# A message-passing kernel on one core: the dot product over vector components moves from the scatter matmuls to VectorE

## The reference

```
h = relu(layernorm(x))                       # then per node: xs (64), xv (32 x 3), two small linear maps
w = silu(edge_embed @ fc_w1 + b1) @ fc_w2 + b2          # 192 weights per edge: 64 + 64 + 32 + 32
m0_a = w_ss * xs[src] * sh0                              # 64 scalars
m1_a = (w_sv * xs[src])[:, :, None] * sh1[:, None, :]    # 64 vectors
m1_b = w_vs[:, :, None] * xv[src] * sh0                  # 32 vectors
m0_b = w_vv * einsum('emc,ec->em', xv[src], sh1) / sqrt(3)   # 32 scalars: a dot product over c
agg = segment_sum(concat(m0_a, m0_b, m1_a, m1_b), dst)
out = x + h + gated(agg @ W2 + h @ Wsc)      # W2_s: 96 x 96, W2_v: 96 x 32, silu gates
```

## Time and profile before

| | |
|---|---|
| median of 3 runs | 825.63 us (825.25 to 831.32) |
| the profiled execution, whole | 822.46 us |
| its span, first to last instruction | 820.8 us |
| TensorE passes | 5900 |
| TensorE matmul busy, weight load busy | 648.3 us, 544.9 us |
| VectorE, GpSimd, ScalarE busy | 348.5 us, 405.1 us, 183.8 us |
| mean granted TensorE clock | 0.543 of full speed |

### The profile page before, as it was taken

How to read it: one execution, slowest core, us unless ns; L and a number is a source line. 1 busy time by engine, 2 the same in 40 slices (tenths; PEclk the granted TensorE clock), 3 DMA queues, 4 the chain that set the end, 5 groups by cost and what they waited for, 6 DMA issues and landing times.

```text
span 820.8 us, 16769 instructions
## 1 busy us (share of the span) xinstructions
PE 648.3 (79%) x5900; PEld 544.9 (66%) x5900; DVE 348.5 (42%) x1126; ACT 183.8 (22%) x357; POOL 405.1 (49%) x434
## 2 busy tenths in 40 slices
PE   6656776877797797797789789779778978977877
PEld 6535665666676686686577668668667766866766
DVE  7412444433454443444345434434343443444435
ACT  4611112212121212112212212121221221212121
POOL 2374555545554644554554455545556455544630
PEclk9755556555655555555555555555555555555657
DMA  9621111112111211211211211112212121111210
GB/s 297 165 71 41 52 49 53 46 50 57 48 49 49 65 40 49 63 41 49 57 44 48 53 48 52 52 42 57 56 46 54 45 57 48 49 53 44 57 39 13
DMA packets 38783, 48.10 MB, mean 59 GB/s; under 512 B 9908, under 2 KB 31443, under 8 KB 38379
## 3 DMA queue, kind: packets, MB, share of 16 engines
q0 software_dynamic: 20160, 34.33, 15.8%
q1 hardware_dynamic: 18193, 13.46, 5.5%
q10 hardware_dynamic: 410, 0.07, 0.1%
HBM read 40.67 MB, written 4.00 MB: 54 GB/s over the span
## 4 chain that ended last, share of the span: by engine, by line
PE 59%; another core or an unknown queue 17%; issue 11%; DVE 7%; DVEq 1%; ACT 0%; ACTq 0%
PE ps L701 20%; PE ps L691 15%; PE ps L682 7%; PE ps L696 7%; PE ps L733 3%; PE ps L697 2%; DVE agg L592 2%; DVE P L555 2%; PE ps L726 2%; PE ps L731 1%; PE ps L727 1%; PE ps L673 1%; DVE M L535 1%; DVEq L577 1%
## 5 line engine op out<-in xcount | busy, mean ns | idle before, releaser
L463 POOL DMA_INDIRECT gath<-table,src_sb x416 | 396.4, 953 | 362.1 <-DVE P L555 255.2
L701 PE MATMUL ps<-S,P 128*64 128x32 f32 x2496 | 294.7, 289 | 60.6 <-issue 60.1
L701 PEld LDWEIGHTS ps<-S,P 128*64 128x64 f32 x2496 | 273.2, 218 | 67.3 <-issue 66.8
L696 PE MATMUL ps<-S,P 128*64 128x48 f32 x832 | 180.9, 317 | 55.4 <-DVE agg L592 53.8
L696 PEld LDWEIGHTS ps<-S,P 128*64 128x64 f32 x832 | 122.3, 206 | 102.7 <-DVE agg L592 60.2
L691 PE MATMUL ps<-fc_sb,hid 64*128 64x192 f32 x832 | 180.8, 557 | 9.1 <-issue 8.6
L697 PE MATMUL ps<-S,P 128*64 128x16 f32 x832 | 148.2, 256 | 10.1 <-issue 10.1
L496 ACT ACTIVATE hid<-ps,fb_sb 128x256 f32<-128x256 f32 x104 | 49.4, 475 | 450.0 <-PE ps L682 294.9
L691 PEld LDWEIGHTS ps<-fc_sb,hid 64*128 64x128 f32 x832 | 121.2, 311 | 43.4 <-issue 42.6
L550 DVE TENSOR_TENSOR P<-ps,gath 128x512 f32<-128x512 f32 x103 | 71.0, 690 | 167.8 <-PE ps L691 63.0
L697 PEld LDWEIGHTS ps<-S,P 128*64 128x64 f32 x832 | 136.5, 222 | 6.1 <-issue 5.6
(11 more groups left out here) (90 smaller groups left out, 260.9 us busy)
## 6 DMA issues: line engine op xcount, KB each, us to landing
gath<-table,src_sb POOLq DMA_INDIRECT x416, 3.5
agg<-zeros SPq DMA_DIRECT2D x3, 1024.0 KB, 12.4
emb<-emb_t SPq DMA_DIRECT2D x104, 24.0 KB
out<-res SPq DMA_DIRECT2D x24, 78.1 KB
x_sb<-x SPq DMA_DIRECT2D x5, 350.0 KB
table<-prod SPq DMA_DIRECT2D x3, 420.0 KB
sh_sb<-sh_t SPq DMA_DIRECT2D x1, 840.0 KB, 8.0
table<-prod SPq DMA_DIRECT2D x1, 280.0 KB
```

What stands on the lines that cost most here:

```text
L463: nc.gpsimd.indirect_dma_start(gath[:, u, j, :], None, table, bass.IndirectOffsetOnAxis(ap=src_sb[:, t:t + 1], axis=0)).then_inc(landed, 16)
L696: nc.tensor.matmul(oj[0:64, :, 0:3], pj[:, 64:128], sj[:, :, 1:4], start=True, stop=True)
L701: ins = nc.tensor.matmul(oj[64:128, :, c:4:3 - c], pj[:, lo:lo + 64], sj[:, :, 0:2 + c:1 + c], start=(c == 0), stop=(c == NC - 1), skip_gr ...
```

## The change

The selectors S get a fifth column, the bare match, and `sh` is laid out as (x, y, z, scalar). VectorE computes for each edge the dot product of the gathered vectors with x, y, z: a multiplication into `xsh` (384 elements per partition) and a sum over the components into `dot` (128 elements), in a new function `dots` that stands between the adds and the products of a step and does not wait for the weights. P shrinks to 256 columns: `w_ss xs`, `w_sv xs`, `w_vs xv` for three components, and `w_vv dot`. The scatter of a tile takes four matmuls: two write partitions 0 to 63, two write partitions 64 to 127, in alternating order, and none accumulates. The sums of the vectors lie in other partitions than before, so the output weights `wo_v` are laid out four times over, and `sums_part` still has four matmuls, two of them now with 64 output columns in place of 32. The separate tile M of matches is gone, and with it a wait on `p_S`; waits on `p_xsh` and `p_dot` are new.

```diff
--- before.py
+++ after.py
-PC = 320
+PC = 256
...
-        wo_v = sb("wo_v", [VD, V0])
+        wo_v = sb("wo_v", [128, 2, 2, V0])
...
-        M = sb("M", [128, QT, WIN])
-        S = sb("S", [128, 2, QT, WIN, 4])
+        S = sb("S", [128, 2, QT, WIN, 5])
...
-            (wo_v[:, :], w2v), (wo_s[0:S0, :], w2s[0:S0, :]), (wo_s[96:128, :], w2s[S0:96, :]),
+            (wo_v[0:VD, 0, 0, :], w2v), (wo_v[96:128, 0, 1, :], w2v[S0:VD, :]),
+            (wo_v[0:S0, 1, 0, :], w2v[0:S0, :]), (wo_v[S0:VD, 1, 1, :], w2v[S0:VD, :]),
+            (wo_s[0:S0, :], w2s[0:S0, :]), (wo_s[96:128, :], w2s[S0:96, :]),
...
+                nc.gpsimd.memset(wo_v[:, :, :, :], 0.0)
...
-                nc.vector.memset(ps[64:96, 0:4, 0:2 * NTN], 0.0).then_inc(s_pz, 1)
+                nc.vector.memset(ps[64:128, 6, 0:QT * WIN * AC], 0.0)
+                nc.vector.memset(ps[64:128, 0:4, 0:QT * WIN * AC], 0.0).then_inc(s_pz, 1)
...
+        xsh = sb("xsh", [128, QT, NC, V0])
+        dot = sb("dot", [128, QT, V0])
...
-                    def matches(q):
-                        t = q * QT
-                        if not (isinstance(q, int) and q == 0):
-                            dve.wait_ge(p_S, q)
-                        nc.vector.tensor_tensor(M[:, :, :], iota[:, :].unsqueeze(1).broadcast_to([128, QT, WIN]),
-                                                dstrel[:, bass.ds(t, QT)].unsqueeze(2).broadcast_to([128, QT, WIN]),
+                    def matches(q, u):
+                        nc.vector.tensor_tensor(S[:, u % 2, :, :, 4],
+                                                iota[:, :].unsqueeze(1).broadcast_to([128, QT, WIN]),
+                                                dstrel[:, bass.ds(q * QT, QT)].unsqueeze(2).broadcast_to([128, QT, WIN]),
                                                 ALU.is_equal).then_inc(p_M, 1)

                     def selectors(q, u):
                         dve.wait_ge(p_M, q + 1)
                         nc.vector.tensor_tensor(
-                            S[:, u % 2, :, :, :], M[:, :, :].unsqueeze(3).broadcast_to([128, QT, WIN, 4]),
+                            S[:, u % 2, :, :, 0:4], S[:, u % 2, :, :, 4].unsqueeze(3).broadcast_to([128, QT, WIN, 4]),
                             sh_sb[:, bass.ds(q * QT, QT), :].unsqueeze(2).broadcast_to([128, QT, WIN, 4]),
                             ALU.mult).then_inc(p_S, 1)

+                    def dots(i, q, u, j0=0, j1=QT):
+
+                        if not (isinstance(i, int) and q == NQ - 1):
+                            dve.wait_ge(p_gath[u], (i + 1) * (16 * QT))
+                        nc.vector.tensor_tensor(
+                            xsh[:, j0:j1, :, :], gath[:, u, j0:j1, S0:D].rearrange("p j (c m) -> p j c m", c=NC),
+                            sh_sb[:, bass.ds(q * QT + j0, j1 - j0), 0:NC].unsqueeze(3).broadcast_to([128, j1 - j0, NC, V0]),
+                            ALU.mult).then_inc(p_xsh, 1)
+                        dve.wait_ge(p_xsh, q + 1 + j0)
+
+                        if not (isinstance(q, int) and q == 0 and j0 == 0):
+                            dve.wait_ge(p_prod, q + j0)
+                        nc.vector.tensor_reduce(dot[:, j0:j1, :], xsh[:, j0:j1, :, :].rearrange("p j c m -> p j m c"),
+                                                AX.X, ALU.add).then_inc(p_dot, 1)
+
                     def products(i, q, u):
-                        dve.wait_ge(p_gath[u], (i + 1) * (16 * QT))
                         dve.wait_ge(p_w, q + 1)
                         w, g, pu = w_ps(u), gath[:, u, :, :], P[:, u % 2, :, :]
                         nc.vector.tensor_tensor(pu[:, :, 0:128].rearrange("p j (a m) -> p j a m", a=2),
                                                 w[:, :, 0:128].rearrange("p j (a m) -> p j a m", a=2),
                                                 g[:, :, 0:S0].unsqueeze(2).broadcast_to([128, QT, 2, S0]), ALU.mult)
-                        for a in range(2):
-                            lo = 128 + V0 * a
-                            ins = nc.vector.tensor_tensor(
-                                pu[:, :, 128:PC].rearrange("p j (c a m) -> p j c a m", c=NC, a=2)[:, :, :, a, :],
-                                w[:, :, lo:lo + V0].unsqueeze(2).broadcast_to([128, QT, NC, V0]),
-                                g[:, :, S0:D].rearrange("p j (c m) -> p j c m", c=NC), ALU.mult)
-                        ins.then_inc(p_prod, 1)
+                        nc.vector.tensor_tensor(
+                            pu[:, :, 128:128 + VD].rearrange("p j (c m) -> p j c m", c=NC),
+                            w[:, :, 128:160].unsqueeze(2).broadcast_to([128, QT, NC, V0]),
+                            g[:, :, S0:D].rearrange("p j (c m) -> p j c m", c=NC), ALU.mult)
+                        dve.wait_ge(p_dot, q + 1)
+                        nc.vector.tensor_tensor(pu[:, :, 128 + VD:PC], w[:, :, 160:WN], dot[:, :, :],
+                                                ALU.mult).then_inc(p_prod, 1)

                     def last_products(j):
                         u = SLOTS - 1
                         dve.wait_ge(p_last[j], 16)
+                        dots(NI - 1, NQ - 1, u, j, j + 1)
                         dve.wait_ge(p_w, NQ)
                         w, g, pj = w_ps(u)[:, j, :], gath[:, u, j, :], P[:, u % 2, j, :]
                         nc.vector.tensor_tensor(
@@ -568,10 +591,12 @@
                             w[:, 0:128].rearrange("p (a m) -> p a m", a=2),
                             g[:, 0:S0].unsqueeze(1).broadcast_to([128, 2, S0]), ALU.mult)
                         nc.vector.tensor_tensor(
-                            pj[:, 128:PC].rearrange("p (c a m) -> p c a m", c=NC, a=2),
-                            w[:, 128:WN].rearrange("p (a m) -> p a m", a=2).unsqueeze(1).broadcast_to([128, NC, 2, V0]),
-                            g[:, S0:D].rearrange("p (c m) -> p c m", c=NC).unsqueeze(2).broadcast_to([128, NC, 2, V0]),
-                            ALU.mult).then_inc(p_prod, 1)
+                            pj[:, 128:128 + VD].rearrange("p (c m) -> p c m", c=NC),
+                            w[:, 128:160].unsqueeze(1).broadcast_to([128, NC, V0]),
+                            g[:, S0:D].rearrange("p (c m) -> p c m", c=NC), ALU.mult)
+                        dve.wait_ge(p_dot, NQ + j)
+                        nc.vector.tensor_tensor(pj[:, 128 + VD:PC], w[:, 160:WN], dot[:, j, :],
+                                                ALU.mult).then_inc(p_prod, 1)
...
-                                matches(q + 2)
+                                matches(q + 2, u)
...
+                        dots(i, q, u)
                         products(i, q, u)
...
-                        nc.tensor.matmul(oj[0:64, :, 0:3], pj[:, 64:128], sj[:, :, 1:4], start=True, stop=True)
-                        nc.tensor.matmul(oj[0:64, :, 3], pj[:, 0:64], sj[:, :, 0], start=True, stop=True)
-
-                        for c in range(NC):
-                            lo = 128 + 64 * c
-                            ins = nc.tensor.matmul(oj[64:128, :, c:4:3 - c], pj[:, lo:lo + 64], sj[:, :, 0:2 + c:1 + c],
-                                                   start=(c == 0), stop=(c == NC - 1), skip_group_check=True)
+                        nc.tensor.matmul(oj[0:64, :, 0:3], pj[:, 64:128], sj[:, :, 0:3], start=True, stop=True)
+                        nc.tensor.matmul(oj[64:128, :, 0], pj[:, 128:192], sj[:, :, 3], start=True, stop=True)
+                        nc.tensor.matmul(oj[0:64, :, 3], pj[:, 0:64], sj[:, :, 3], start=True, stop=True)
+
+                        ins = nc.tensor.matmul(oj[64:128, :, 1:4:2], pj[:, 192:PC], sj[:, :, 3:5], start=True, stop=True)
                         return ins

                     def scatter(q, u):
...
                         nc.tensor.matmul(o[:, 0:96], sums[3], wo_s[:, :], start=False, stop=False, skip_group_check=True)
-                        for k in range(NC):
-                            ins = nc.tensor.matmul(o[:, 96 + V0 * k:96 + V0 * (k + 1)], sums[k][0:VD, :], wo_v[:, :],
-                                                   start=False, stop=(k == NC - 1), skip_group_check=True)
+                        nc.tensor.matmul(o[:, 96:160], sums[0], wo_v[:, 0, :, :].rearrange("p a k -> p (a k)"),
+                                         start=False, stop=False, skip_group_check=True)
+                        nc.tensor.matmul(o[:, 128:192], sums[1][0:VD, :],
+                                         wo_v[0:VD, 1, :, :].rearrange("p a k -> p (a k)"),
+                                         start=False, stop=False, skip_group_check=True)
+                        ins = nc.tensor.matmul(o[:, 160:192], sums[2][0:S0, :], wo_v[0:S0, 0, 0, :],
+                                               start=False, stop=True, skip_group_check=True)
...
-    sh = np.pad(a["edge_attr_4"], ((0, pad + QT * TE), (0, 0)))
+
+    sh = np.pad(a["edge_attr_4"][:, [1, 2, 3, 0]], ((0, pad + QT * TE), (0, 0)))
```

(8 more changed lines are left out.)

## The result

The changed kernel takes 847.62 us (median of 4 runs, 841.63 to 848.83) against 825.44 us before (4 runs, 823.17 to 831.32): ratio 1.028, 95% interval 1.021 to 1.035. It is slower; the forecast was 720 us, range 702 to 772.

A forecast was written before the change was run, and what follows sets the result against it. It took TensorE to be bound at one pass per 0.134 us on average. From the profiled 822.5 us, minus 111 for passes, plus 4 and 2, gave 717; adjusted to the runs' median, 720 us, range 702 to 772.

The forecast's parts named there:

- the first term of the sum: TensorE's scatter: 832 of 5900 passes fewer, at an average 0.134 us per pass with stops included, 111 us less.
- GpSimd: ... Nothing: Gathers, 5.0 us per quad: above TensorE's 4.2 but under the average step of 5.9, so no cost.
- the scatter: TensorE's scatter of one step after the change: length near 1.8 us, against 2.57 before.
- the reduction: VectorE's new sum of 384 elements into 128 per step: 0.57 us, bounds 0.28 and 1.14.
- VectorE's step: VectorE's step without a wait after the change: 4.15 us, against TensorE's 4.2.
- Its share: VectorE's busy share of the span after the change: near 55%, from 42%.
- The streams' saving: TensorE's two scatter streams, four passes per tile each: 0.77 us less per step, 80 us over 104 quads.
- Rival B: TensorE's stops keep their number and length; only the streams' 80 us come out: 762 us, chance 0.28.
- Rival C: The scatter's two halves do not run side by side; 53 us saved: 777 us, chance 0.08.
- D: VectorE becomes the bound if the strided sum costs 1.4 us: no change, 825 us, chance 0.07.
- E: Selectors at 20-byte steps make TensorE's scatter passes take twice 0.107 us: 88 us more, 914 us, chance 0.05.
- Slower: Whole kernel slower by over 1%: chance 0.05.

The follow-up runs named there:

- e12: Kernel before, GpSimd waiting for free slots only at every second quad, so gathers go in runs of 8: 908.78 us, ratio 1.103.
- e7: Kernel before with every second gather left out, products reading old rows: 592.67 and 619.85 us where the kernel before takes 820.87.
- e5: The changed kernel as it is, measured again where the kernel before takes 578.25 us: 577.29 us, ratio 1.000.
- e4: Changed kernel with every second gather left out, products reading old rows: 556.32 us.
- e14: Changed kernel, a quad's gathers also waiting for the end of the scatter four quads before: 578.26 us, ratio 1.000 to the kernel before.
- e17: Kernel before, a quad's gathers also waiting for the end of the scatter four quads before: 750.26 us, ratio 0.907.
- e16: Changed kernel, gathers also waiting for the scatter four quads before, run where the kernel before takes 826.37 us: 730.71 us, ratio 0.886.
- e10: Changed kernel, a quad's gathers starting when three of the four before have landed: 760.22 us, ratio 0.922 to the kernel before.
- e18: Changed kernel with a GpSimd memset ahead of each gather: four runs, 785.68, 788.42, 817.74 and 884.36 us.
- e9: Changed kernel, a semaphore per gather, each starting when the one two before has landed: 700.40 us, ratio 0.850 to the kernel before.
- e13: Kernel before, a semaphore per gather, each starting when the one two before has landed: 706.04 us where the kernel before takes 578.88.

## Why the prediction was wrong

- **The failed step** is the first term of the sum, "one pass per 0.134 us on average", with "GpSimd: ... Nothing" beside it. The constancy in the earlier trace rows was real, but passes were not its cause: they were just what a step holds. After the change it is 847.55/5068 = 0.167 us per pass of the whole execution, for 822.46/5900 = 0.139 before. The stops went with unbroken runs of gathers instead: e12 makes more of them with no change in compute, and e7 takes nearly all away with all passes in place. Why the change made more runs is read from the timelines, and no run varied the step alone: their number hangs on whether GpSimd finds the next slot free when its fourth gather is out, that is on whether a compute step is shorter than 5.0 us. In the kernel before a step is 4.95 us and longer with a node tile, close to that limit, and 46 quads had a run of their own; at 4.2 us two have. By this reading the shorter step was itself the trigger.
- **GpSimd's 5.0 us** was written down as "above TensorE's 4.2 but under the average of 5.9". The average was an outcome of the stops. Where there are none GpSimd is the floor: 416 x 1.25 = 520 us, and the ratio is 1.000 (e5).
- **Right in size**: 5068 passes; the scatter, 1.85 us for 1.8; the reduction, 0.594 us for 0.57; VectorE's step, 4.18 us for 4.15. Its share is 50% and not 55, as the span did not shrink. The streams' saving was 0.86 us for 0.77: the forecast's 2.57 us for the scatter before ends at 420.88, where no row stands, and to the next hidden layer it is 2.71 (421.01 in the earlier trace rows). With half the gathers, TensorE's saving can be seen in the time: 556 us (e4, free) against 593 and 620 (e7, held), where the forecast's streams gave 80. The kernel before was granted a mean clock of 0.651 and 0.602 in those two runs, the changed one 0.529 in e4, which may be where the rest of the saving went; no run at one clock shows it.
- **Rival B** came nearest (stops do not go with passes) but kept their number; the runs of eight went from 26 to 48. Rival C fell: both halves start at 430.19 and a tile of eight passes takes 0.43 us. Weight loads and matmuls overlap too, with all on 128 rows: their busy times are 56% and 68% of one span. The sentence on row groups in the Trainium skill, "TensorE: Matmul & The Clock Gate", section Part 3 (The mechanism), does not describe that. Rivals D and E fell with 0.594 us for the reduction that reads 128 bytes from element to element, and 0.107 us per pass of the scatter over 20-byte steps; the penalty for crossing 16 bytes that "SBUF — State Buffer", section Door 1 (The DMA port swizzle), names is not seen in either: the reduction is 0.04 us longer than the product of as many elements in the changed kernel (0.551), and the lower stream before had the same 0.11 us per pass. "Slower" had 0.05, all of it for E, the wrong mechanism.
- **What was there to read**: the rows [9] gave the spacing, and the waits that end in "remote" end 2.7 to 3.1 us behind a last gather in each window of the earlier trace rows. I had asked where in the loop stops sit, and how many passes lie between, but not which engine's work ends with them.

## What to carry to other kernels

When several engines stop together and the trace shows no reason, lay the other engines' timelines beside the end of the stop, those off the chain too: the one whose work ends there each time is the suspect, and a constant average of anything else is no cause. Before a compute step is made shorter than what the engine that issues gathers needs, ask what becomes of the pauses it had. A wait that ties gathers to the compute engine's own progress cost nothing in a free series (e14) and in held ones took 9% off the kernel before (e17) and 14% off the changed one (730.71 against 847.62, in two series).

## What the runs showed of the hardware

- In held series, TensorE's signals are seen late while GpSimd's indirect gathers follow each other without a pause. In runs of eight the last ones are mostly seen 2.6 to 3.0 us after the start of the last gather, up to 8.0 us after their pass (a scatter that ended about 432.1 was heard of at 440.07). Those early in a run come on time: the scatter that ended at 421.08, 0.7 us into the run from 420.38, was answered by VectorE at 421.23. In e16 and e17, with runs of four and 2.5 to 2.8 us from the last start to the next, they are 2.65 and 2.0 us late; with the shorter pause of e10 up to 8.1 us, and with gathers 1.35 us apart (e18) some are seen within the run.
- VectorE's signals come through within a run: in the kernel before, the second product of the pair

```profile
424.12 1.01 DVE L555 TENSOR_TENSOR P<-ps,gath 128x384 f32<-128x384 f32 x2
```

ends at 425.13, and GpSimd's fifth gather of the run starts with it at 425.40. In the runs of eight of the changed kernel many of VectorE's records are missing, so there it is not shown.
- The gather's median from issue to landing differs with it; the page of the changed kernel in the held series, then of e5:

```profile
gath<-table,src_sb POOLq DMA_INDIRECT x416, 3.7
```

```profile
gath<-table,src_sb POOLq DMA_INDIRECT x416, 2.6
```

The row of a gather (0.95 us) ends long before that. The Trainium skill, "Perfetto Trace Analysis", section DMA Instruction — SWDGE (GPSIMD), says that such an instruction's end in the profile is the end of descriptor writing, not of the movement; the two numbers agree.
- What makes a series held or free stays open. Two chips gave both, in different series; within a series nothing changed it; kernels and inputs were the same. Why TensorE's signals and not VectorE's are late was not tried either, nor which part of a gather (its descriptors, its movement, its own semaphore) holds them up. e9 was seen in a held series alone, e13 in a free one, and e17 in a held one.
